# A 16-head attention stage: the next pair's row maxima issued ahead of the subtraction of the maximum

## What is computed

```python
k = (kv_input @ Wk).reshape(b, f + q_len, HEADS, DIM_HEAD).transpose(0, 2, 1, 3)
v = (kv_input @ Wv).reshape(b, f + q_len, HEADS, DIM_HEAD).transpose(0, 2, 1, 3)
q = q * SCALE
sim = jnp.einsum('bhqd,bhfd->bhqf', q, k)
sim = sim - jax.lax.stop_gradient(jnp.max(sim, axis=-1, keepdims=True))
alphas = jax.nn.softmax(sim, axis=-1)
out = jnp.einsum('bhqf,bhfd->bhqd', alphas, v)
return out @ Wo
```

## Time and profile before

| | |
|---|---|
| three runs, median (lowest to highest) | 760.79 us (760.69 to 764.2) |
| profiled execution, span | 761.9 us |
| PE busy | 610.9 us, 80% of the span |
| the chain that ended last | PE 57%, DVE 28% of the span |
| DVE, ACT, POOL busy | 569.0, 324.3, 417.5 us |
| the stage's first score product to its last subtraction | 414.3 to 646.1 us |

### The profile page before, as it was taken

One profiled execution on the slowest core, in us unless ns is written; L12 is line 12 of the kernel. 1 busy time (PEld: TensorE's weight loads), 2 busy tenths in 40 slices (PEclk: granted clock), 3 DMA queues, 4 the chain that ended last, 5 costly groups with the idle time before them and its releaser, 6 DMA issues.

```text
span 761.9 us, 15577 instructions
## 1 busy us (share of the span) xinstructions
PE 610.9 (80%) x5721; PEld 387.8 (51%) x5721; DVE 569.0 (75%) x1043; ACT 324.3 (43%) x565; POOL 417.5 (55%) x349
## 2 busy tenths in 40 slices
PE   6399756798468658838428899999999998799997
PEld 5277522354244335325313456666666665566766
DVE  4837899659969985995976777667667766489887
ACT  2433200231132132113213787767858766455661
POOL 5424254417636652769593756656656666346652
PEclk9999977769779858965556999999999999989999
DMA  7311100000000000003310000000000000000001
GB/s 190 90 34 29 55 1 0 0 2 1 0 2 0 0 0 0 0 0 97 96 28 0 2 2 2 2 2 2 2 2 2 2 2 2 1 1 0 0 0 28
DMA packets 14163, 12.95 MB, mean 17 GB/s; under 512 B 3120, under 2 KB 11936, under 8 KB 14112
## 3 DMA queue, kind: packets, MB, share of 16 engines
q1 hardware_dynamic: 14112, 12.25, 5.6%
HBM read 11.72 MB, written 0.52 MB: 16 GB/s over the span
## 4 chain that ended last, share of the span: by engine, by line
PE 57%; DVE 28%; issue 7%; ACT 3%; POOL 3%; DVEq 1%; DMA 1%; ACTq 0%; SPq 0%; POOLq 0%; PEld 0%
DVE work L717 5%; PE banks L1034 5%; PE banks L1712 5%; DVE work L775 4%; PE banks L1041 4%; PE banks L950 3%; PE banks L465 3%; PE banks L1059 3%; PE banks L1019 2%; PE banks L952 2%; PE banks L951 2%; PE banks L1067 2%; PE banks L1422 2%; PE banks L1061 2%; PE banks L1060 2%
## 5 line engine op out<-in xcount | busy, mean ns | idle before, releaser
L1361 POOL TENSOR_TENSOR attn<-work,attn 128x512 f16<-128x512 f32 (+1 forms) x96 | 141.9, 1481 | 94.8 <-ACT attn L1160 94.8
L1250 DVE TENSOR_REDUCE nmax<-banks 128x2 bf16<-128x1024 f32 x64 | 78.3, 1223 | 21.5 <-PE banks L1019 21.3
L717 DVE TENSOR_TENSOR work<-banks,gatev 128x512 f32<-128x512 f32 x120 | 79.3, 684 | 15.8 <-PE banks L467 15.3
L465 PE MATMUL banks<-weights,xbTh 128*128 128x512 f16 x120 | 50.7, 422 | 28.2 <-DVE work L717 26.7
L1469 POOL TENSOR_SCALAR work<-work 128x512 f16<-128x512 f32 x64 | 53.0, 851 | 35.7 <-ACT work L1401 33.1
L1159 ACT ACTIVATE work<-banks,maskbias 128x512 f32<-128x512 f32 x64 | 44.3, 692 | 59.7 <-PE banks L1041 59.7
L845 POOL TENSOR_TENSOR work<-work 128x512 f32<-128x512 f32 x24 | 30.5, 1269 | 66.6 <-DVE work L717 64.6
L1407 DVE TENSOR_TENSOR work<-work 128x512 f16<-128x512 f32 x64 | 57.1, 949 | 12.2 <-POOL work L1469 12.2
L1712 PE MATMUL banks<-ident,work 128*128 128x128 f32 x276 | 53.3, 331 | 8.5 <-DVE work L1912 3.0
L490 PE MATMUL banks<-attn 64*128 64x256 f16 x64 | 22.1, 360 | 47.0 <-ACT work L631 37.9
L1059 PEld LDWEIGHTS banks<-work,attn 128*128 128x128 f16 x512 | 46.8, 97 | 18.8 <-POOL attn L1361 10.8
(11 more groups left out here) (275 smaller groups left out, 1922.2 us busy)
## 6 DMA issues: line engine op xcount, KB each, us to landing
stage<-in_L_ffn_w SPq DMA_DIRECT2D x8, 512.0 KB, 3.9
stage<-in_L_ffn_Wkv SPq DMA_DIRECT2D x4, 640.0 KB, 3.9
stage<-in_L_ffn_Wq SPq DMA_DIRECT2D x2, 640.0 KB, 5.1
xt<-in_x SPq DMA_DIRECT2D x1, 512.0 KB, 4.2
ct<-in_ctx SPq DMA_DIRECT2D x1, 512.0 KB, 5.5
wo<-in_L_xattn_Wo SPq DMA_DIRECT2D x1, 512.0 KB
stage<-in_L_xattn_Wv SPq DMA_DIRECT2D x1, 512.0 KB, 3.7
stage<-in_L_xattn_Wq SPq DMA_DIRECT2D x1, 512.0 KB, 3.5
```

Of the source, the lines that this page charges most:

```text
L465: pe.matmul(o, xh, wh, start=True, stop=False)
L717: dve.tensor_tensor(heads8(m.prod[:, k, e, :]), heads8(bank_pj[c % 2][:, :]), wide(g, DH1), ALU.mult).then_inc(s.prod_ready, 1)
L1250: dve.tensor_reduce(m.nmax[:, p % 2, i, :], banks[:, 6:8, :], AX.X, ALU.max, negate=True).then_inc(s.c_max_done, 1)
L1361: pool.tensor_tensor(m.Pl[:, p % 2, kts, :], m.Pf[:, kts, :], m.Ph[:, p % 2, kts, :], ALU.subtract).then_inc(s.c_P_lo, 1)
```

## The change

`scores_T` is split: the score products stay, and the four subtracting products with their wait become `less_max`. In a step, `row_max` of the next pair is now called between the two, for each half.

```diff
                             q = (m.q2h, m.q2h, m.q2l)[x][r, p % 4, :]
                             pe.matmul(pair[h][:, k * S:(k + 1) * S], key, q, start=(k == 0 and x == 0), stop=False)
+
+            def less_max(it, p, half):
+
+                pair = bank_kq[2 * half:2 * half + 2]
                 if half == 0:
                     pe.wait_ge(s.c_max_done, it * PAIRS + (2 * p + 2))
                 for h in range(2):
...
                 scores_T(it, t, 0)
                 if t + 1 < STEPS_C:
                     row_max(it, t + 1, 0)
+                less_max(it, t, 0)
                 if "c" in jobs:
                     job(it, (t, "c"), jobs["c"])
                 scores_T(it, t, 1)
                 if t + 1 < STEPS_C:
                     row_max(it, t + 1, 1)
+                less_max(it, t, 1)
                 for place in "fh":
```

## The result

The changed kernel took 774.84 us, median of 4 runs (772.11 to 780.06), against 760.74 us of the kernel before beside it (4 runs, 759.64 to 764.2): the ratio is 1.0156, with a 95% interval of 1.0114 to 1.0198. It is slower, by 14.1 us where 9.0 were forecast.

The account below looks back on a forecast made before the run. PE's own sequence was taken to bound the attention stage, and a ring of ACT, DVE and PE after the change. 7.0 us from step 5 on plus 2.0 before gave +9.0 on 760.8: 769.8 us, range 764 to 775.5.

Parts of the forecast that it names:

- The saving: Attention stage, PE: two fewer changes of kind in each of 60 halves, 0.09 to 0.10 us each, 11.5 us of PE time.
- The rule on draining: PE in the attention stage: changes of tiling mode drain the engine, so all 11.5 us are kept, 749 us; chance 0.07.
- The ring: Attention steps: exponentials, keys' high and low parts, `take_out`, row maxima, subtraction, exponentials; 7.61 and 7.13 us, 765 to 774; chance 0.74.
- The first five steps: Start of the attention stage: 2.0 us added, with 0.5 and 3 as bounds.
- The 1.1 us for step 2: Step 2's first exponential comes 1.1 us late, since step 1's second subtraction waits with `row_max` for DVE.
- stalls in steps 2 to 4: Attention steps 2 to 4 add 0.3 to 0.5 us each, less what stalls in them absorb.
- From step 29 on: Step 29 to the attention stage's end: the chain runs through the same work as before, so nothing is added.
- Signs that I named: Trace after: PE waits for `take_out` some 14 us, is 87 to 90% busy; no first `row_max` wait directly behind a projection.
- the wait itself: PE before the first half's row maxima: 0.58 us in an even step, about 0.8 us in an odd one.
- Rival 4, the clock: Attention stage: PE's waits lower the granted clock in part of it, about 5 us more, 775 and over; chance 0.10.

Follow-up runs that it names:

- The doubling: `take_out`'s multiplication done twice, the first time into a scratch tile: in the changed kernel 781.23 us, in the kernel before 772.79 us.
- e8: The changed kernel with one useless 128x256 f32 product on DVE right ahead of `take_out` in every step: 812.12 us, ratio 1.0648 to the kernel before.

## Why the prediction was right, and where it was off

**The saving** was costed right: 0.09 to 0.10 us for a change of kind, two fewer per half, 0.20 us, as 1.07 and 0.87 us between scores and job show. The rule on draining that spoke for 749 us holds as to the gap and not as to the time, since PE only waited longer. Where the waits allow it to be kept (the second half alone), steps 5 to 29 are 6.4 us shorter.

**The ring** was right in kind and in size. Steps: 7.61 summed and 7.62 measured, 7.13 and 7.13 (7.22 in the last step of a batch, whose mask column I had overlooked: 0.09 us, three times), 8.90 and 8.80 with a projection. Steps 5 to 29 were to lose 7.0 us and lost 6.4, the projection steps being 0.1 better each. That it is this ring and no other follows, for steps 5 to 29, from four kernels: the first half alone makes the loss (184.2 us), an earlier high part of the keys takes it away (173.5), and 0.33 us added to `take_out` come back 18 times in the changed kernel and 0.2 us in all in the kernel before.

**The first five steps** were too small in the sum: 2.0 taken, 2.6 measured from the first subtraction on. The 1.1 us for step 2 was right in size (6.98 + 7.98 against 5.42 + 8.47 from the first subtraction of step 0 to that of step 2, 1.07), and only in part for the reason given. The sum left step 1's first exponential where it was; yet its subtraction now waits with the first row maxima for the keys' low part, and comes 6.98 us behind that of step 0, where it was 5.42. With the first half alone (e1) this makes 0.45 of the 1.07; the second half's subtraction, which the prediction named, makes the rest. Wrong was that stalls in steps 2 to 4 would absorb part of what they add: they added 0.56, 0.48 and 0.50 us in full. The doubling points to the reason: `take_out` was on the path of these steps already, with no reserve behind it.

**From step 29 on** I had nothing. The first two profiles differ there by 1.2 us, but the second profile of the kernel before took as long as the changed one, 17.1 us both. Step 30 was granted 1.00 in the first profile of the kernel before, 0.80 in the second and 0.79 in both of the changed kernel. Where the changed kernel's step 30 had the full clock, in the profile with `take_out` doubled, the stretch took 16.1 us with 0.33 of doubling in it, against 15.9: that is the clock and not the change.

**The total**: 9.0 forecast; 14.1 in the first set of four runs each, 10.0 in the set of 6 and 17. The stage accounts for 9.2 to 10.4 us whichever profiles are paired. The difference between the sets is in stretches that the change leaves alone, and the profiles show them moving by more than that (408.5 to 419.5 us ahead of the stage). The range 764.0 to 775.5 held the median.

**Signs that I named**: L1019 waits for `take_out`, 14 us said, 12.8 found from 450 to 650 and 14.5 from 416 to 660; the wait itself, the gap between scores and row maxima less its 0.11, is 0.7 us behind an even step without a projection (0.58 said) and 0.9 to 1.0 behind an odd one (about 0.8 said); PE at 91% where 87 to 90 were said; the step behind a projection starts without a wait (its first row maxima stand 0.11 us behind the scores); the values no longer wait for the maximum in odd steps, where they start 0.41 us behind its end, while in even ones they still start 0.15 behind it (13 waits from 450 to 650, 4.1 us). Rival 4, the clock, didn't come: 1.00 in the stage's steady part. I had the line of `take_out`'s last instruction wrong, L1275 for L1277.

**Open**: why a stage that is 6 us shorter (the second half alone, in all steps or in the middle ones) hardly shows in the time. The granted clock takes a good part of the gain, behind the stage in the profile and over the whole span in the timed runs; for equal clock some 2 to 4 of the 6 us are left, by the estimate. Whether the lower clock comes with the shorter stage or by chance isn't shown: the changed kernel, whose stage is longer, was granted 0.885 on the mean in its six runs, and with `take_out` doubled 0.889, where the kernel before beside them had 0.887.

## What to carry to other kernels

Before an instruction is moved behind a wait, ask what that wait releases now and what it would release then: here the saving of 0.2 us per half was real, but it moved ACT's input behind a release that ACT itself starts a step earlier, and a ring of ACT, DVE and PE became the step. Sum such a ring from the rows before believing a busy share of 99.9%; PE's share said nothing of it. And a change in order can be worth taking in one of two places only: in steps 5 to 29 the half whose wait is short gained the 6.4 us that both together lost. Here that gain could not be told from nothing in the whole kernel's time, so it is a gain of the stage and not yet of the kernel.

## What was unexpected of the hardware

- A DVE operation with both inputs in SBUF, and a plain f32 copy from SBUF to SBUF, stood still while POOL worked: 1.36 us at the median where 0.415 is its time alone, and 1.22 where the shortest took 0.34. The same size with one operand out of PSUM took 0.42 us beside the same POOL work. The Trainium skill says why ("SBUF — State Buffer", SBUF: two separate sides): DVE and GpSimd share one pair of ports under an exclusive lock, held for a whole instruction. The trace agrees: each of the 31 copies ends 0.15 us after an instruction of POOL, and each of the 31 products of e8 0.28 us after one.
- The granted clock of the same stretches differs from execution to execution. The last stretch of the kernel before took 85.8 us at 0.99 and 88.9 at 0.96; the part ahead of the attention stage took 408.5 and 414.3, and 408.5 to 419.5 over the fourteen profiles here, in which it is the same code. A saving of 6 us inside one stage is of the same size.
